# Six key/value buffers, later dots and later key scaling beside an on-chip sort

## The reference

```
xn  = layernorm(x)
gnn = two layers: agg = segment_sum(xn[col], row); h = (x + agg/deg) @ W.T + b; silu(layernorm(h))
q, k, v = split(xn @ w_qkv.T)            # 8 heads of 64
k, v = instance_norm(k), instance_norm(v) # over the 64 of a head
dots = einsum("bhnd,bhne->bhde", k, v)    # one 64 x 64 matrix per head, summed over all rows
mix  = (einsum(q, dots) / N) @ w_out.T + b_out
x = x + gnn + mix
x = x + ffn(layernorm(x))                 # experts, chosen by a softmax over the mean row
```

## Time and profile before

| | |
|---|---|
| median of 3 runs | 2919.98 us (2918.04 to 2920.64) |
| profiled execution | 2923.55 us, of it span 2921.8 us |
| mean granted TensorE clock | 0.954 |
| PE busy | 2512.2 us (86%) |
| DVE busy | 1878.7 us (64%) |
| ACT busy | 1402.6 us (48%) |
| POOL busy | 199.0 us (7%) |
| sort: first transposes of round 0, last stage of round 13 | 211.12 us, 537.32 us |

### The profile page before, as it was taken

The page is one execution under the profiler, slowest core; times in us unless marked ns, Lnnn a source line. Parts: engine busy times, 40 slices in busy tenths (PEclk is TensorE's granted clock), DMA queues, the critical chain, the costliest instruction groups (busy, mean ns, idle before and its releaser), DMA issues. The chain is left out here.

```text
span 2921.8 us, 50327 instructions
## 1 busy us (share of the span) xinstructions
PE 2512.2 (86%) x14013; PEld 1458.1 (50%) x14013; DVE 1878.7 (64%) x4792; ACT 1402.6 (48%) x3753; POOL 199.0 (7%) x185
## 2 busy tenths in 40 slices
PE   0877677685889888889999999997999999969997
PEld 0444444332334343334378888883444444445665
DVE  8898887899999999999953222221333333366555
ACT  0877566265777667687821211211222222246665
POOL 0000000000000000000011111100111111115000
PEclk9998899698999999999999999998999999979999
DMA  5000000022245344243275555556444444410000
GB/s 182 19 15 15 11 15 15 17 76 76 89 146 185 116 162 161 103 165 136 102 256 185 157 162 165 157 162 208 140 135 140 141 135 141 140 33 15 22 22 31
DMA packets 167927, 318.02 MB, mean 109 GB/s; under 512 B 30227, under 2 KB 139540, under 8 KB 167764
## 3 DMA queue, kind: packets, MB, share of 16 engines
q1 hardware_dynamic: 115860, 230.55, 24.7%
q10 hardware_dynamic: 51776, 85.24, 8.0%
q0 software_dynamic: 128, 0.26, 0.1%
HBM read 203.09 MB, written 112.92 MB: 108 GB/s over the span
## 5 line engine op out<-in xcount | busy, mean ns | idle before, releaser
L1255 PE MATMUL banks<-outer,ring 128*128 128x512 f16 x2450 | 540.0, 380 | 18.6 <-DMA outer<-table,heavy 11.6
L866 ACT ACTIVATE ring<-banks 128x512 f16<-128x512 f32 (+1 forms) x637 | 365.6, 574 | 291.0 <-POOLq L696 287.9
L1252 PE MATMUL banks<-tabs,ring 128*128 128x257 f16 x2250 | 495.0, 274 | 3.3 <-DMA ring<-counts 3.3
L1253 PE MATMUL banks<-tabs,ring 128*128 128x256 f16 x2250 | 494.9, 273 | 0.0
L1255 PEld LDWEIGHTS banks<-outer,ring 128*128 128x128 f16 x2450 | 240.2, 98 | 299.8 <-issue 23.1
L867 ACT ACTIVATE banks<-banks 128x512 f32<-128x512 f32 (+1 forms) x637 | 367.0, 576 | 0.0
L1951 DVE TENSOR_SCALAR ring<-val,outer 128x512 f16<-128x512 f16 x1102 | 315.1, 345 | 20.0 <-PE banks L1218 19.9
L1218 PE MATMUL banks<-ring 128*128 128x512 f16 x920 | 261.4, 393 | 41.4 <-DVE ring L1951 20.1
L893 ACT ACT_TABLE_LOAD x50 | 64.2, 1283 | 377.7 <-DVE row_stats L2005 377.7
L1252 PEld LDWEIGHTS banks<-tabs,ring 128*128 128x128 f16 x2250 | 220.6, 98 | 31.8 <-issue 4.0
L1253 PEld LDWEIGHTS banks<-tabs,ring 128*128 128x128 f16 x2250 | 220.5, 98 | 25.8
(11 more groups left out here) (391 smaller groups left out, 3816.7 us busy)
## 6 DMA issues: line engine op xcount, KB each, us to landing
counts<-ring ACTq DMA_DIRECT2D x84, 896.0 KB, 4.1
ring<-counts SPq DMA_DIRECT2D x94, 800.0 KB, 4.7
ring<-counts SPq DMA_DIRECT2D x94, 768.0 KB, 4.1
outer<-in_fw SPq DMA_DIRECT2D x8, 1024.0 KB, 8.2
outer<-in_x SPq DMA_DIRECT2D x5, 1280.0 KB, 13.5
x_transposed<-xT SPq DMA_DIRECT2D x50, 128.0 KB, 1.7
outer<-in_x SPq DMA_DIRECT2D x25, 256.0 KB, 3.0
xT<-x_transposed SPq DMA_DIRECT2D x25, 256.0 KB, 2.8
```

The source lines that it names most:

```text
L866: act.activation(held[:, b, 0:q, c, :], cell_bank.rearrange("p (q r) -> p q r", r=P), ACT.Copy, scale=0.25).then_inc(s_cell, 1)
L1252: mm(o[:, 0:D + 1], a, xtab[l][:, COLUMN[cb], D:2 * D + 1], start=cb == 0, stop=False)
L1253: m = mm(o[:, 0:D], a, xtab[l][:, COLUMN[cb], 0:D], start=False, stop=cb == NT - 1)
L1255: m = mm(o, a, xtab[l][:, COLUMN[cb], 0:2 * D], start=cb == 0, stop=cb == NT - 1)
```

## The change

Three things, and the list of windows with them.

1. `kv` has six buffers in place of four. The two new ones take the place in the ring tile (columns 4096 to 6144) where squares of two tiles in four were written; the squares of all tiles now go to one scratch `squared`, and ACT waits for the squares of the tile before. Before DVE writes field 1 over that part of the ring tile it waits for the dots of the tiles held there.
2. PE's dots come behind a tile's product, up to two tiles' dots at a time, and no further than the tiles of the window before the previous one. In the row phase DVE scales five ticks behind the sums in place of three. `kv_stds` in the rounds moves from the head of the window to behind the first tile's first squares.
3. In the rounds `kv_scales` always stands behind the round's last signal.

The tiles of the rounds are dealt out as 0, 4, 1, 3, 1, 3, 2, 3, 2, 3, 2, 4, 1, 3 in place of 0, 4, 0, 4, 0, 4, 0, 4, 1, 4, 2, 4, 3, 2.

```diff
-SCALE_LAG = 3
-WINDOWS = [2] * ROW_WINDOWS + [0, 4, 0, 4, 0, 4, 0, 4, 1, 4, 2, 4, 3, 2]
+SCALE_LAG = 5
+KV_RING = 6
+WINDOWS = [2] * ROW_WINDOWS + [0, 4, 1, 3, 1, 3, 2, 3, 2, 3, 2, 4, 1, 3]
...
-        kv_sq = [tabs[:, 0:1024], tabs[:, 1024:2048], ringf[:, 4096:5120], ringf[:, 5120:6144]]
+        kv[2:2] = [ringf[:, 4096:5120], ringf[:, 5120:6144]]
+        in_ring = max(t for t in range(NT) if t % KV_RING in (2, 3)) + 1
+        assert in_ring <= WSTART[ROW_WINDOWS + ROUNDS - 2]
+        squared = tabs[:, 0:1024]
...
             def kv_copies(t):
-                if t >= 4:
-                    act.wait_ge(s_dots, t - 3)
+                if t >= KV_RING:
+                    act.wait_ge(s_dots, t - KV_RING + 1)
...
             def kv_squares(t, half):
+                w = window_of(t)
                 if half == 0:
-                    if t >= 4:
-                        act.wait_ge(s_kvr, windows_before(window_of(t - 4) + 1))
+                    if windows_before(w) >= 2:
+                        act.wait_ge(s_kvr, windows_before(w) - 1)
+                    if t:
+                        act.wait_ge(s_kvq, t)
                     act.wait_ge(s_kvc, 2 * t + 2)
...
-                    if t == WSTART[w] and 0 < w < ROW_WINDOWS:
+                    if t == WSTART[w] and w and w != ROW_WINDOWS + 1:
                         kv_stds(w - 1)
...
-                if n:
-                    kv_stds(ROW_WINDOWS + n - 1)
                 window(ROW_WINDOWS + n)
...
                 for t in range(WSTART[w], WSTART[w + 1]):
-                    dots_to(t - 4)
                     first_product(t)
                     kv_product(t)
-                dots_to(WSTART[w])
+                    dots_to(min(dotted + 2, WSTART[max(w - 1, 0)]))
...
-                scales_late = n % 2 == 0 and WINDOWS[before + 1] == 0
                 for j in stages:
...
-                    if n and not scales_late and j == stages[1]:
-                        kv_scales(before)
                 if n < ROUNDS - 1 and n % 2 == 0:
                     ins.then_inc(s_rows, 1)
-                if n and scales_late:
+                if n == ROUNDS - 1:
+                    link(ins)
+                if n:
                     kv_scales(before)
-            link(ins)
...
+            dve.wait_ge(s_dots, in_ring)
             dve.tensor_scalar(field_i[1], ki, KC_SH, P - 1, op0=ALU.arith_shift_right, op1=ALU.bitwise_and).then_inc(s_dec, 1)
```

More of the change, by code:

```diff
@@ L770, in kv_copies @@
             def kv_copies(t):
-                if t >= 4:
-                    act.wait_ge(s_dots, t - 3)
+                if t >= KV_RING:
+                    act.wait_ge(s_dots, t - KV_RING + 1)
                 for h in range(2):
                     act.wait_ge(s_kvp, 2 * t + h + 1)
-                    act.activation(kv[t % 4][:, h * 512:(h + 1) * 512], bank[4 + h], ACT.Copy).then_inc(s_kvc, 1)
+                    act.activation(kv[t % KV_RING][:, h * 512:(h + 1) * 512], bank[4 + h], ACT.Copy).then_inc(s_kvc, 1)
             def kv_squares(t, half):
+                w = window_of(t)
                 if half == 0:
-                    if t >= 4:
-                        act.wait_ge(s_kvr, windows_before(window_of(t - 4) + 1))
+                    if windows_before(w) >= 2:
+                        act.wait_ge(s_kvr, windows_before(w) - 1)
+                    if t:
+                        act.wait_ge(s_kvq, t)
                     act.wait_ge(s_kvc, 2 * t + 2)
-                w = window_of(t)
                 k = windows_before(w) % 2 * 160 + (t - WSTART[w]) * 16
                 for g in range(half * HEADS, (half + 1) * HEADS):
-                    ins = act.activation(kv_sq[t % 4][:, g * DH:(g + 1) * DH], kv[t % 4][:, g * DH:(g + 1) * DH], ACT.Square,
+                    ins = act.activation(squared[:, g * DH:(g + 1) * DH], kv[t % KV_RING][:, g * DH:(g + 1) * DH], ACT.Square,
                                          accum_out=msc[:, k + g:k + g + 1])
@@ L1036, in dots @@
                 pe.wait_ge(s_kn, t + 1)
-                b = kv[t % 4]
+                b = kv[t % KV_RING]
                 for pr in range(PAIRS):
@@ L1590, in kv_scales @@
                     dve.wait_ge(s_kvc, 2 * t + 2)
-                    kg = kv[t % 4][:, 0:512].rearrange("p (g e) -> p g e", e=DH)
+                    kg = kv[t % KV_RING][:, 0:512].rearrange("p (g e) -> p g e", e=DH)
                     dve.tensor_tensor(kg, kg, msc[:, k:k + 8].unsqueeze(2).to_broadcast([P, 8, DH]), op=ALU.mult).then_inc(s_kn, 1)
```

## The result

| | before | after |
|---|---|---|
| median | 2919.98 us (2918.04 to 2923.71, 5 runs) | 2903.23 us (2902.41 to 2904.75, 5 runs) |
| profiled execution, its span | 2923.55, 2921.8 | 2902.41, 2900.7 |
| keys of the row phase ready | 211.07 | 220.73 |
| rounds, from there to L1673 | 327.51 | 301.25 |

The ratio is 0.9944 (95% interval 0.9933 to 0.9955): 16.8 us faster by the medians, 13 to 20 by the interval, where 22.0 (2898.0) was forecast. In the two traces the span fell by 21.1 us: the trace of before is an execution 3.6 us above its median. Of these 21.1, the row phase cost 9.7, the rounds gave 26.3, the first piece behind the sort 2.9, and all that follows it 1.6.

A forecast was written before the change was run, and what follows sets the result against it. VectorE's sort was taken as the bound, idling 48.4 us at turns mostly for ACT. Terms -24.3 (turns), +1.5 (added windows) and +0.8 (row phase) gave -22.0 us, from median 2919.98 to 2898.0, range 2889 to 2910.

The forecast's parts named there:

- What bounds the kernel, and the rounds: Rounds: VectorE idles 48.4 us at turns, most made late by ACT; 24.1 stays, 24.3 saved, less 1.5 for added windows.
- The worked-out gaps: VectorE's gaps at turns: 5.8, 4.2, 7.3, 5.9, 3.5, 3.84 us behind rounds 2 to 12; 1.5 behind rounds 3 to 9.
- Scaling behind the signal: Turns of the rounds: VectorE scales keys instead of idling, at 0.22 us per window plus 0.65 per tile.
- The rival's 11 us: Rounds: gain from hidden scaling alone, six windows of 18 tiles, 13 us less 1.5, if idle only moves; chance 0.15.
- I take 0, by rows 9: Row phase: the 8.7 us wait before the reciprocal reappears before the sums, so gain 0; bounds 0 and -8.7.
- 0.8 us for the added semaphore: Row phase: each tile's squares wait for one more semaphore, 0.06 us per tile on 13 tiles; bounds 0 and 1.
- The sign named for it: Row phase: ends at 211 to 212 us, no reciprocal wait, more idle before the sums, about 12 us together.
- The first piece behind the sort: After the sort: what follows moves as a whole, with 0.65 us of one more scaling on VectorE's path to this piece.
- The moved idle: Rounds: tiles taken from odd rounds overrun even ones by as much, leaving only hidden scaling: 2909 us; chance 0.15.
- the row phase's gain: Row phase: ACT gains from earlier dots as VectorE does, so 8.7 us more is saved: 2889.3 us; chance 0.10.
- The slower rival: Rounds: PE's idle stretches keep it at 1.2 GHz, products included, some 60 us more: 2958 us; chance 0.05.
- The transposes don't lift the clock: Even rounds: first products run at half rate after transposes, 7 us lost in rounds 4, 6, 8, 10: 2905; chance 0.05.

The follow-up runs named there:

- The experiment: The kernel after, with DVE's scaling of keys put before the last stage in rounds 3, 5 and 7 to 13: 2916.95 us, ratio 0.9990.
- the last kernel: The kernel after with row-phase dots behind the second tile, another deal of tiles, and matmuls of zeros in row phase and rounds: 2874.71 us, ratio 0.9845.

## Why the prediction was right, and which step failed

*What bounds the kernel, and the rounds.* Right. The waits for dots went from 42.9 to 2.2 us. The worked-out gaps have the measured pattern, long behind rounds 2, 6 and 8, 1.5 behind odd ones; the rounds lost 26.3 us where 22.8 was worked out. The excess is in the turns to 9 (5.9, measured 4.60), 2, 5, 7, 11 and 12. The turn behind round 2 was 0.8 us worse: its root stood late on ACT, and the scaling of four tiles began 3.83 us behind the signal.

*Scaling behind the signal.* Right, and so is the price. The rival's 11 us are for six windows of 18 tiles, less 1.5. The experiment moves nine windows of 19 tiles, for which the prediction's prices (0.22 a window, 0.65 a tile) give 14.3 us, and it cost 13.7.

*Row phase: failed.* The step was "I take 0, by rows 9" with 0.8 us for the added semaphore. It measured 9.7 us. That the 8.7 us before the reciprocal would come back before the sums was right for the larger part (in the kernel before with the later scaling 5.7 us came back and 2.7 were gained). The sign named for it, a row phase that ends at 211 to 212 us with about 12 us before the sums, did not come: it was 220.73 and 22.8. The term for the place of the dots is missing from the sum, and what I missed is in the diff: I read PE's dots as standing in the same place in a row-phase window, two tiles' worth between the products. They had stood behind the second, where PE would otherwise idle, and moved in front of it. That costs ACT 0.7 us per window by the order and 1.65 by the clock, as PE's idle at the head grew from 2.4 to 4.0 us. The rows with 3.98 and 3.99 us of idle and the slow half products behind them show it, and the run with the dots put back takes 8.5 of the 9.7 us away. The kernel before paid for its own 2.4 us of idle in some windows too (15.3 to 16.1 us), so the row phase lost less than 2.35 us times its windows.

*The first piece behind the sort,* taken to move as a whole, came 2.9 us shorter: DVE's waits for PE fell by 3.5 us there, PE's clock being higher. *The total was luck in part.* Of the traces' 21.1 us, against 22.0 forecast, the row phase took 8.9 more than worked out; the rounds gave 3.5 more, the first piece 2.9 and the rest 1.6, none of them foreseen, and they happened to make up for it. The trace of before lay 3.6 us above its median and that of after 0.8 below, which is why 21.1 us between traces are 16.8 between medians, 5.2 from the forecast.

*Rivals.* The moved idle and the row phase's gain are both ruled out: the turns behind even rounds overran by no more than worked out, save 0.8 us behind round 2, and the row phase lost. The slower rival had the right cause, PE at 1.2 GHz after idling, in the wrong place: products in the rounds kept 1.88 us nearly throughout, and the row phase paid. *The transposes don't lift the clock* is not borne out: before the turn behind round 3 PE idled 6.04 us, the sixteen transposes took 3.31, between the 1.97 and 3.67 us of turns wholly at either level, and the product right behind them was at 1.03 us, the fast figure (timeline of PE, after). So the clock rose while PE did nothing but transposes. Elsewhere it rose later: behind round 9 (423.91) the transposes took 3.67 us and that product still 1.91.

```profile
293.46 3.31 PE L1008 MATMUL banks<-ident,ring 128*128 128x128 f32 x16 [6.04 <-DVE ring L1481]
...
296.61 1.03 PE L1034 MATMUL banks<-big,xT 128*128 128x256 f32 x4
```

## What to carry to other kernels

When work is moved in one engine's queue, write out the queue before and after for each phase in which the line runs, and ask of each place what idle it filled. Work that nobody waits for (here the dots) is best put where its engine would idle, not between two things that another engine waits for. On PE such filler also held the clock for what came next, and even work of no use paid: four matmuls of zeros a window took the time from 2903.23 to 2891.28 us. It has to end before the work that others wait for: in the last kernel it delayed one turn by 1.0 us.

## What was not expected of the hardware

The same idle of 2.3 us did not decide PE's clock: with two matmuls of zeros it fell behind it in three of the five windows between 118.15 and 198.16 us and held in two, all in one execution, while in the row phase it held each time behind 0.55 us and fell each time behind 4.0. In the kernel before, 2.4 us left the half product at 1.88 us in four windows of six. With the two matmuls of zeros the loss came whole or not at all, 1.65 us per window; in other kernels its size varied (15.3 and 15.4 us for 14.3 before, and 17.52 for 16.65 after). Keeping PE at work through the rounds raised its granted clock there from 0.89 to 0.97 and shortened them by 10.4 us with no change in what DVE or ACT compute.
